# Two heads' key products issued in turn into four PSUM banks, in a linear attention and mixture-of-experts kernel on one core

## The reference, cut to what matters

```
x = x + attn(layernorm(x))     # gated delta rule, 16 heads of 64, 1024 channels
x = x + ffn(layernorm(x))      # softmax attention of 16 heads of 8, then a mixture of 8 experts, top 2
```

```
S_t = alpha_t * (S_{t-1} - beta_t k_t (k_t^T S_{t-1})) + beta_t k_t v_t^T ;   o_t = q_t^T S_{t-1} + D (q_t . k_t) v_t
```

## Time and profile before

| | us |
|---|---|
| median of three runs | 7937.8 (7932.78 to 7957.76) |
| profiled execution, span from first to last instruction | 7946.7 |
| TensorE matmuls busy | 6133.5, 77% |
| VectorE busy | 4732.0, 60% |
| ScalarE busy | 3013.4, 38% |
| GpSimd busy | 2662.6, 34% |
| mean granted TensorE clock | 0.703 of full |

### The profile page before, as it was taken

How to read it: one execution, slowest core, us unless ns; L and a number is a source line. 1 busy time by engine, 2 the same in 40 slices (tenths; PEclk the granted TensorE clock), 3 DMA queues, 4 the chain that set the end, 5 groups by cost and what they waited for, 6 DMA issues and landing times.

```text
span 7946.7 us, 128119 instructions
## 1 busy us (share of the span) xinstructions
PE 6133.5 (77%) x41472; PEld 4339.3 (55%) x41472; DVE 4732.0 (60%) x11688; ACT 3013.4 (38%) x5573; POOL 2662.6 (34%) x2989
## 2 busy tenths in 40 slices
PE   5787877877877778778787777787777877878777
PEld 3555554555545655546555456554565545655555
DVE  5655566655566555665556765556655566555662
ACT  2333334433344433343333443334333334333343
POOL 3333223433233332333322343323433233332331
PEclk6677666776667776667776677666777667766667
DMA  1000000000000000000000000000000000000000
GB/s 61 2 2 3 3 2 2 3 3 3 2 2 3 3 3 3 2 2 2 3 3 2 2 3 3 3 2 2 3 3 3 3 2 2 2 3 3 2 2 3
DMA packets 26490, 30.22 MB, mean 4 GB/s; under 512 B 4072, under 2 KB 22768, under 8 KB 25328
## 3 DMA queue, kind: packets, MB, share of 16 engines
q1 hardware_dynamic: 25712, 20.49, 0.8%
HBM read 16.29 MB, written 4.19 MB: 3 GB/s over the span
## 4 chain that ended last, share of the span: by engine, by line
PE 43%; issue 29%; POOL 15%; DVE 9%; ACT 3%; POOLq 1%; SPq 0%; DVEq 0%; ACTq 0%; DMA 0%
PE bank L852 42%; POOL NP L589 4%; POOL Gam L617 4%; POOL Gam L614 3%; POOL NP L586 2%; DVE NP L1245 2%; DVE NP L1378 2%; DVE hn L1231 1%; POOL NP L592 1%; PE bank L856 1%; POOL frstd L655 1%; ACT Gam L743 1%; ACT NP L689 1%; DVE Gam L1397 1%; DVE lpp L1265 0%
## 5 line engine op out<-in xcount | busy, mean ns | idle before, releaser
L852 PE MATMUL bank<-QK 64*128 64x256 f32 (+1 forms) x4096 | 1378.4, 466 | 260.0 <-ACT pT L815 108.5
L852 PEld LDWEIGHTS bank<-QK 64*128 64x128 f32 (+1 forms) x4096 | 611.4, 183 | 863.3 <-ACT pT L815 262.8
L1245 DVE SCALAR_TENSOR_TENSOR NP<-bank,conv_w,NP 128x255 f32<-128x255 f32 (+2 forms) x2304 | 929.6, 471 | 78.1 <-ACT NP L689 78.1
L839 ACT ACTIVATE QK<-bank,b 128x256 f32<-128x256 f32 x1024 | 422.7, 470 | 1176.5 <-PE bank L852 1175.0
L852 PE MATMUL bank<-mT,W 128*128 128x256 f32 x2048 | 671.0, 489 | 0.1
L852 PE MATMUL bank<-xnT,Wqkv 128*128 128x256 f32 x1536 | 583.3, 527 | 108.5 <-DVE NP L1245 53.5
L1563 DVE SCALAR_TENSOR_TENSOR moe<-bank,wsel,moe 128x128 f32<-128x128 f32 x512 | 156.1, 347 | 847.4 <-PE bank L852 847.4
L852 PE MATMUL bank<-NP,head_cols 128*32 128x256 f32 x1536 | 206.8, 484 | 498.3 <-POOL NP L586 498.2
L852 PE MATMUL bank<-W,QK 128*128 128x128 f32 x4096 | 538.0, 287 | 22.5 <-DVE moe L1563 22.5
L743 ACT COPY Gam<-NP 32x256 f32<-32x256 f32 x512 | 321.1, 627 | 612.3 <-DVE fac L1385 607.8
L852 PEld LDWEIGHTS bank<-W,QK 128*128 128x128 f32 x4096 | 525.9, 203 | 47.8 <-DVE moe L1563 28.6
(11 more groups left out here) (211 smaller groups left out, 11626.7 us busy)
## 6 DMA issues: line engine op xcount, KB each, us to landing
xin<-in_x SPq DMA_DIRECT2D x33, 128.0 KB, 2.1
out<-moe SPq DMA_DIRECT2D x32, 128.0 KB, 1.8
W<-in_W SPq DMA_DIRECT2D x1, 2048.0 KB
NP<-in_c_q_sel SPq DMA_DIRECT2D x1, 1536.0 KB, 8.7
NP<-in_c_k_sel SPq DMA_DIRECT2D x1, 1536.0 KB, 11.9
NP<-in_c_alpha_sel SPq DMA_DIRECT2D x1, 1024.0 KB, 5.4
Wqkv<-in_Wq SPq DMA_DIRECT2D x1, 512.0 KB, 12.7
Wqkv<-in_Wk SPq DMA_DIRECT2D x1, 512.0 KB, 13.2
```

The costliest lines, as they stand in the source:

```text
L839: ins = s.activation(h1[:, n % 2, f, :], ps[:, q, :], ACT.Gelu_apprx_tanh, bias=b1[:, n, f:f + 1])
L852: return mm(out_, lhsT, rhs, start=first, stop=last)
L1245: v.scalar_tensor_tensor(acc[:, n % 2, m, j:T], ps[:, m, 0:T - j], conv_w[:, kind, c, PAD - j:KT - j], acc[:, n % 2, m, j:T], ALU.mult, AL ...
```

## The change

The decay broadcast gets one bank (4) for all heads, and the key products get four (0 to 3, `h % 4`). TensorE goes over the eight pairs of heads: it issues the four products of the pair with the even and the odd head in turn, chunk by chunk, and after the pair the decay broadcasts of the next odd and the next even head, each followed by the `ffn` steps of its milestone. The broadcast of head 0 is issued ahead of the loop. VectorE's program, the number of products and their shapes stay.

```
-        g += [(("alpha", h), h % 2, "v_Gam", h + 1), (("kk", h), 2 + h % 2, "v_NP", h + 1)]
+        g += [(("alpha", h), 4, "v_Gam", h + 1), (("kk", h), h % 4, "v_NP", h + 1)]
...
-                for h in range(H):
-                    c, rows = h // 2, rows_of(h)
+                def decay(h):
                     if reused(i, ("alpha", h)):
                         pe.wait_ge(*free_at(i, ("alpha", h)))
                     ps = bank(("alpha", h))
                     pe.wait_ge(v_alpha.sem, v_alpha.at(i, 7))
                     product(ps[:, 0:NT * GW], alpha_sel[:, h * P:(h + 1) * P],
                             alpha3[:].rearrange("p t w -> p (t w)")).then_inc(full(("alpha", h)), 1)
-                    if reused(i, ("kk", h)):
-                        pe.wait_ge(*free_at(i, ("kk", h)))
-                    ps = bank(("kk", h))
+
+                decay(0)
+                for c in range(NC):
+                    both = (2 * c, 2 * c + 1)
+                    for h in both:
+                        if reused(i, ("kk", h)):
+                            pe.wait_ge(*free_at(i, ("kk", h)))
                     pe.wait_ge(v_QK.sem, v_QK.at(i, c + 1))
                     for t in range(NT):
-                        ins = product(ps[:, t * T:(t + 1) * T].rearrange("p (a k) -> p a k", a=2),
-                                      QK[rows, c, 1, TOK[t]], QK[rows, c, :, TOK[t]])
-                    ins.then_inc(full(("kk", h)), 1)
-                    meanwhile(("head", h))
+                        for h in both:
+                            rows = rows_of(h)
+                            ins = product(bank(("kk", h))[:, t * T:(t + 1) * T].rearrange("p (a k) -> p a k", a=2),
+                                          QK[rows, c, 1, TOK[t]], QK[rows, c, :, TOK[t]])
+                            if t == NT - 1:
+                                ins.then_inc(full(("kk", h)), 1)
+                    for h in both:
+                        if h + 1 < H:
+                            decay(h + 1)
+                        meanwhile(("head", h))
```

## The result

The change makes the kernel faster. Its median is 7691.6 us (7666.2 to 7709.9, four runs) against 7937.8, a ratio of 0.9677 with an interval of 0.9654 to 0.9700. By the ratio that is 7681, 256 us less than before, where 176 less were forecast, and 9 us under the low end of the range (7690); the plain median, 7691.6, lies 2 us inside, and the interval takes in both. Ratios here leave out runs more than 1.5% above the fastest of their kernel: two of this kernel's eight on a second chip (7811 and 7845.5) and one of its six on a third (12612).

A forecast was written before the change was run, and what follows sets the result against it. No single engine bounds the whole; in the heads stage VectorE does at full clock, TensorE at half clock alone. Savings of 177 us over all batches gave 7770 from the span, about 7761 from the median; forecast 7762, range 7690 to 7890.

The forecast's parts named there:

- the rows side by side: Heads stage, TensorE: a pair's four products take the time of two, 2.00 us at half clock, 1.06 at full.
- the loop at half clock: Heads stage: scan, broadcasts and pair close a loop of 3.52 us a pair, against 4.66 before.
- the block stage: Stage behind the heads stage: stays at about 43.06 us, so the earlier end of the heads stage passes on.
- VectorE hides the wait; a pair costs the same: Heads stage at full clock: new loop of 2.34 us lies below VectorE's 2.90 for two heads, so no gain there.
- 17 batches x 5.1 + 10 x 6.5 + ...: Heads stages of all batches, grouped by their clock before the change: savings sum to 177 us.
- the clock rises in the stage: Rival, heads stage: denser work raises the clock for some two more pairs a batch, 50 us less, 7710; chance 0.10.
- the clock's 50 us: Heads stage: further saving if the clock rises there, giving 7710 us; chance 0.10.
- the later stages' 45: Stages between block and next heads: lower bound, 1.5 us less in each, -45 us.
- The later stages: Between block and next heads, 162.8 us each: no mean change taken, bounds -45 and +90 us.

The follow-up runs named there:

- order inside a pair: Changed kernel with both products of the even head ahead of both of the odd one, banks as changed; ratio 0.9646 to the kernel before, 7714.7 us.
- three banks: Kernel before, head by head, with three banks for the key products and two for the decay broadcast; ratio 0.9915, 7884.7 us.
- the banks alone: Kernel before with four banks for the key products and one for the broadcast, product after product as before; ratio 0.9642, 7705.4 us.
- two kernels with banks and pairs: Changed kernel with the even head's products first (0.9646), and with the next pair's first chunk between the two broadcasts (0.9643, 7702.6 us).
- the order alone: Changed kernel with the old banks, two for key products and two for broadcasts, pairs still in turn; ratio 1.0075, 8045.5 us.
- the copy: Two-element VectorE copy after each scan: in the changed kernel 0.9761, 7732.3 us; in the kernel before with the new banks 0.9902, 7881.0 us.
- the last variant: Changed kernel with three product banks, two broadcast banks, both broadcasts ahead of each pair and four idle bf16 products a pair; 0.9520, again 0.9508 (7580.6 us).
- two and three banks: Changed kernel with three product banks, two broadcast banks and both broadcasts of a pair ahead of its products, no idle products; ratio 0.9788, 7841.2 us.
- denser pairs: Changed kernel with four more bf16 products ahead of each pair, their results overwritten; ratio 0.9653, 7669.8 us.

## Why the prediction was right and wrong

*Right: the rows side by side.* Forecast 2.1 and 1.1 us for a pair's eight matmuls, measured 2.08 and 1.14. The trace of the kernel before could have told: the prediction says that it "has no two products on different rows and equal columns", but behind the block stage it has these, 16 matmuls on partitions 0 to 63 into one bank, then 16 on 64 to 127 into another:

```profile
4094.36 3.39 PE L852 MATMUL bank<-S,QK 64*128 64x64 f32 x32 [0.69 <-ACT S L775]
```

On one set of rows they start 0.11 us apart. The first of the second set starts at 4095.754, 6 ns after the 13th of the first set and ahead of its last three. The Trainium skill (TensorEngine Tiling (Array Packing), Performance Considerations) warns that tiling doesn't speed up the emptying of PSUM. These runs agree: at full clock the kernel without any overlap has the same 1.37 us a head as the changed one.

*Right: the loop at half clock.* 3.52 forecast and measured, 8 us saved forecast in batch 0, 9.5 measured, and 8.5 where batch 0 ran at 0.50 throughout (32.42, order inside a pair). *Right: the block stage* (43.06, now 43.04).

*Wrong: "At full clock one scan follows the next after 1.45 us ... and VectorE has no idle time", so that "VectorE hides the wait; a pair costs the same".* This is the step that failed: it priced the full-clock part at nothing. The 1.45 was a loop through the two product banks. The rows show it: the load of head h at 3982.34, the broadcast behind it at 3983.41 (the trace), the scan at 3983.73, then the multiplications 0.61 after the scan, 0.85 long, and 0.06 to the load of head h+2: 1.07 + 0.32 + 0.61 + 0.85 + 0.06 = 2.91 for two heads. The bracket in the earlier trace rows names the wait, 0.29 for VectorE to free a bank; I read it as TensorE having time to spare. VectorE's own pace is 1.37, as the kernels with more banks show. In the earlier trace rows the multiplications end at 3983.74 and the scan starts at 3983.73, which looks like an engine at its limit; in the kernels with four banks a scan starts 0.08 us before the multiplications' end (3843.57 + 0.85 = 3844.42 against 3844.34). Rows that just touch hid 0.08 us of waiting a head. By itself that is 0.16 x 4 pairs, 0.6 us a batch, some 20 us in all; the rest of the miss is the next step.

*Wrong: "17 batches x 5.1 + 10 x 6.5 + ...", each batch with its old clock.* This is the mis-sized term: 177 forecast, 258 measured. The 17 went from about 37.7 to about 31.2 (6.5 each, 24 us more in all) and the ten from about 42.7 to about 31.3 (11.4 each, 49 more); the other five give 8. Batch 16 explains it. A mean clock of 0.69 over 37.63 us was 23.3 us at half clock; 0.84 over 31.27 is 10.0. The first slow broadcast (0.40 us) now comes 18.7 us into the stage, at 3850.63, where the first slow products came after 14.3 (3985.24), and before the stage ends the clock is up again (1.00 from 3860.7 on). No batch but batch 0 is below 0.70 now. That whole passes settled at 235.5 us goes with it; what chooses that length is not shown.

*The rival that came nearest* is "the clock rises in the stage", given 0.10 and 7710. Its event, less time at half clock, happened, and its reason only in part: it looked for denser work at half clock, and said that at full clock nothing gets denser. Four more products a pair go with a clock of 1.00, and where heads go one after another through four banks the slower pace loses it (0.94 at 1.37 us a head, 0.69 at 1.44). But with three banks 1.37 us a head has 0.82 and at times 0.50, in pairs the slower pace loses nothing (0.89 at 1.44), and one more product a head, one after another, gains nothing. Why the clock falls where it does stays open. The time fell under the range, by the ratio, because its low end took each bound alone: the clock's 50 us and the later stages' 45 came partly together.

*Not foreseen: what brings the gain.* The prediction credits the products side by side. The runs credit the banks: on one chip the banks alone have 0.9642 and two kernels with banks and pairs 0.9646 and 0.9643; the order alone has 1.0075. Side by side pays some 8.5 us in batch 0 and makes the kernel less dependent on VectorE's pace (0.9761 against 0.9902 with the copy, on two chips). For the rest of the changed kernel it pays nothing that can be measured. Whether it pays in the last variant, with the broadcasts out of its way and the idle products, is not shown: that kernel with its heads one after another was not run. Nor was the table taken apart: no run has four product banks and two broadcast banks, or two and one.

*The later stages* gave 22 us where 0 was forecast, inside the bounds. In the experiments they stood between 22 us under 4997.48 (order alone) and 190 over it (two and three banks), in no proportion to what was edited.

## What to carry to other kernels

Before reordering products to overlap them, give them another bank: follow each wait for a freed bank once round its loop, for a small one (0.29 us here) can pace an engine that seems to have no idle time. Where the granted clock changes inside a loop, a stage's gain can't be summed with each pass's old clock, and whole passes fall into a few lengths: 41 us cut from a stage gave nothing, 45 us of added work made one kernel 0.5% faster, and idle products on TensorE made one 2.7% faster and others not. Judge an edit by its stage's loop at either clock, and the whole by variants on one chip, the ones with idle products among them. When a bank changes hands, look also at what used it in the stage ahead.

## What the runs showed of the hardware

TensorE started a product on free rows ahead of products on occupied rows that had been issued before it: eight matmuls in 1.14 us in the order even, even, odd, odd, the same as in turn. The Trainium skill (TensorE: Matmul & The Clock Gate, Step-by-step: what each phase is for) says that only stationary loads are pulled ahead and that the matmuls themselves stay in program order. By that rule the odd head's products could only have started beside the last of the even head's, and the pair would have taken about 1.6 us (the estimate in that run's expectation); the measurement decides against it for products on separate rows. In the two places looked at (this one at full clock, and the kernel before at 4095.754) the product passed three matmuls, and the last one issued was still the last to start.

The clock stayed at 0.50 beside a TensorE that was busy 46.25 of 47.22 us (three banks, above), and at 1.00 beside one that was busy 22.06 of 30.24 us (denser pairs). One program can run in more than one cycle of its own: 235.5 or 242.4 us a pass in profiles on different chips, and 7681 to 7845 us in all on one.
